# A spectral recurrence with 64 by 64 rotations in place of padded 128 by 128 ones

## The reference

```python
h = _ln(x, ln1_g, ln1_b)
spec = jnp.einsum('bsd,fd->bsf', h, W_to)            # W_to: (64, 128)
real, imag = (spec[..., :32], spec[..., 32:])
decay = sigmoid(log_decay); omega = tanh(frequencies) * 0.1
c, s = cos(omega), sin(omega)
def step(carry, u):                                  # 64 steps in time, 32 sequences at once
    sr, si = carry[0] * decay + u[0] * 0.1, carry[1] * decay + u[1] * 0.1
    nr = clip(sr * c - si * s, -10.0, 10.0)
    ni = clip(sr * s + si * c, -10.0, 10.0)
    return ((nr, ni), (nr, ni))
_, out = scan(step, zeros, (real, imag))
x2 = x + einsum('bsf,df->bsd', concat(out), W_from) * 0.1
return x2 + (gelu(_ln(x2, ln3_g, ln3_b) @ W_ffn1.T + b_ffn1) @ W_ffn2.T + b_ffn2) * 0.1
```

## Time and profile before

| | |
|---|---|
| runs | 3461.35, 3450.01, 3452.66 us; median 3452.66 |
| profiled execution | 3455.96 us, its span 3454.1 us |
| mean granted clock of TensorE | 0.879 |
| busy over the span | PE 79%, PEld 51%, DVE 63%, ACT 44%, POOL 12% |
| the loop over the time steps | 298.4 to 344.7 us of the span |

### The profile page before, as it was taken

One profiled execution on the slowest core, in us unless ns is written; L12 is line 12 of the kernel. 1 busy time (PEld: TensorE's weight loads), 2 busy tenths in 40 slices (PEclk: granted clock), 3 DMA queues, 4 the chain that ended last, 5 costly groups with the idle time before them and its releaser, 6 DMA issues. The chain is left out here.

```text
span 3454.1 us, 66228 instructions
## 1 busy us (share of the span) xinstructions
PE 2724.6 (79%) x26806; PEld 1744.5 (51%) x26806; DVE 2180.4 (63%) x6743; ACT 1514.6 (44%) x2755; POOL 410.8 (12%) x313
## 2 busy tenths in 40 slices
PE   7887543796997899999999999999479757887633
PEld 4656442454665355555555555555245425664422
DVE  4444403575111289999999999996578643445776
ACT  3441311463333245555555555553389422444521
POOL 2320011340000000000000000000059400002200
PEclk9998776797999589999999999996699867999866
DMA  7750041000000101001001000100022102550000
GB/s 164 185 126 10 18 127 28 7 3 15 13 19 23 29 20 30 21 21 30 21 21 29 23 21 22 30 2 1 7 77 98 37 0 68 130 138 20 9 0 12
DMA packets 206592, 142.78 MB, mean 41 GB/s; under 512 B 11778, under 2 KB 195045, under 8 KB 206256
## 3 DMA queue, kind: packets, MB, share of 16 engines
q1 hardware_dynamic: 205264, 136.70, 14.9%
q0 software_dynamic: 1024, 1.85, 0.2%
HBM read 134.31 MB, written 4.46 MB: 40 GB/s over the span
## 5 line engine op out<-in xcount | busy, mean ns | idle before, releaser
L2863 DVE CUSTOM_DVE_ANT_0 L_xattn_junk<-L_xattn_ps_mx,L_xattn_shift 128x512 f32<-128x512 f32 (+1 forms) x1024 | 544.3, 568 | 114.9 <-issue 111.9
L2944 ACT ACTIVATE L_xattn_pT<-L_xattn_ps_st 128x512 f32<-128x512 f32 x768 | 416.9, 594 | 348.1 <-PE L_xattn_ps_st L2728 348.1
L2909 DVE TENSOR_TENSOR L_xattn_pT<-L_xattn_pT,L_xattn_capT 128x512 f32<-128x512 f32 (+1 forms) x896 | 542.0, 645 | 31.5 <-ACT L_xattn_pT L2944 26.6
L2741 PE MATMUL L_xattn_ps_mx<-L_xattn_kT,L_xattn_qb 32*128 32x512 f32 (+1 forms) x2048 | 513.4, 571 | 0.9 <-DVE L_xattn_tops L2863 0.4
L2728 PE MATMUL L_xattn_ps_st<-L_xattn_qb,L_xattn_kT 32*128 32x256 f32 (+1 forms) x3328 | 457.1, 389 | 0.0
L2728 PEld LDWEIGHTS L_xattn_ps_st<-L_xattn_qb,L_xattn_kT 32*128 32x128 f32 (+1 forms) x3328 | 310.4, 186 | 22.8
L2774 PE MATMUL L_xattn_ps_pv<-L_xattn_pT,L_xattn_v 128*17 128x128 f32 x6656 | 271.3, 283 | 0.0
L2774 PEld LDWEIGHTS L_xattn_ps_pv<-L_xattn_pT,L_xattn_v 128*17 128x17 f32 x6656 | 149.7, 98 | 170.6 <-DVE L_xattn_pT L2909 126.6
L1811 DVE SCALAR_TENSOR_TENSOR x<-L_ffn_ps_o,L_ffn_weights,x 128x128 f32<-128x128 f32 x128 | 36.0, 344 | 224.5 <-PE L_ffn_ps_o L1724 224.5
L2741 PEld LDWEIGHTS L_xattn_ps_mx<-L_xattn_kT,L_xattn_qb 32*128 32x128 f32 x2048 | 168.3, 189 | 12.4 <-DVE L_xattn_tops L2863 9.7
L2754 PE MATMUL L_xattn_ps_st<-L_xattn_less,L_xattn_ones_b 3*128 3x512 bf16 x768 | 167.1, 394 | 1.7 <-ACT L_xattn_pT L2944 1.4
(11 more groups left out here) (554 smaller groups left out, 5172.1 us busy)
## 6 DMA issues: line engine op xcount, KB each, us to landing
L_xattn_ctx<-in_ctx SPq DMA_DIRECT2D x96, 768.0 KB
L_attn_cc<-scratch_rows SPq DMA_DIRECT2D x32, 512.0 KB, 3.6
L_xattn_mask<-in_mask_keys SPq DMA_DIRECT2D x32, 400.2 KB, 7.1
L_ffn_w<-in_L_ffn_w SPq DMA_DIRECT2D x32, 256.0 KB, 3.0
L_ffn_w<-in_L_ffn_W SPq DMA_DIRECT2D x16, 256.0 KB, 3.1
L_xattn_mask<-in_mask_pairs SPq DMA_DIRECT2D x32, 100.1 KB, 4.4
L_xattn_ctx<-in_ctx SPq DMA_DIRECT2D x96, 32.5 KB
scratch_in<-L_ffn_zero SPq DMA_DIRECT2D x1, 1024.0 KB, 5.1
```

Source lines behind the costliest of these rows:

```text
L2741: last = nc.tensor.matmul(mx[:, w % 3, to:to + width], qb[n % 3][32 * g:32 * g + 32, 2 * (p % 2):2 * (p % 2) + 2, :].rearrange("p h q -> p ...
L2863: last = nc.vector.tensor_tensor_reduce(out=junk[:, w % 3, to:to + width], in0=mx[:, w % 3, to:to + width], in1=shift[:, k0:k0 + width], s ...
L2909: nc.vector.tensor_tensor(x, x, capT[0:k, j[0]:j[1], :].unsqueeze(2).broadcast_to([k, j[1] - j[0], 4, S]), ALU.min)\
L2944: nc.scalar.activation(pT[b % HELD][:, :, gi, :], st[:, w % 3, :].rearrange("p (c k) -> p c k", c=2), ACT.Exp)\
```

## The change

F2 becomes 64, so that `rot_u` and `rot_z` are 64 by 64, the states, inputs and projections live on 64 partitions, and the five transfers take only the unpadded part. The fillers become matmuls of the 64 by 64 corner of the identity with itself, four for each step as before.

```diff
-    F2 = P
+    F2 = P // 2
@@
-            sp.dma_start(wto[:, :], a[f"{name}_W_toT"]).then_inc(gains, 16)
-            sp.dma_start(raw[:, 0:1], a[f"{name}_decay"]).then_inc(angles, 16)
-            sp.dma_start(raw[:, 1:2], a[f"{name}_freq"]).then_inc(angles, 16)
-            sp.dma_start(halves[:, :], a["c_halves"]).then_inc(angles, 16)
-            sp.dma_start(freq[:, :], a["c_freq"]).then_inc(angles, 16)
-            sp.dma_start(wfrom[:, :], a[f"{name}_W_fromT"]).then_inc(loaded, 16)
+            sp.dma_start(wto[:, :], a[f"{name}_W_toT"][:, 0:F2]).then_inc(gains, 16)
+            sp.dma_start(raw[:, 0:1], a[f"{name}_decay"][0:F2, :]).then_inc(angles, 16)
+            sp.dma_start(raw[:, 1:2], a[f"{name}_freq"][0:F2, :]).then_inc(angles, 16)
+            sp.dma_start(halves[:, :], a["c_halves"][0:F2, :]).then_inc(angles, 16)
+            sp.dma_start(freq[:, :], a["c_freq"][0:F2, :]).then_inc(angles, 16)
+            sp.dma_start(wfrom[:, :], a[f"{name}_W_fromT"][0:F2, :]).then_inc(loaded, 16)
@@
                 for _ in range(SPARE):
-                    nc.tensor.transpose(turn[:, 0, 0:P], c.ident[:, :], c.ident[:, :])
+                    nc.tensor.matmul(turn[0:F2, 0, 0:F2], c.ident[0:F2, 0:F2], c.ident[0:F2, 0:F2], start=True, stop=True)
```

## The result

The changed kernel takes 3481.77 us (median of nine runs, 3463.59 to 3483.67) against 3452.66 (nine runs, 3436.34 to 3461.35). The ratio is 1.008, its 95% interval 1.0056 to 1.0104: slower, by more than the 0.3% that the measurement tells from nothing, and 1.8 us from the 3480.0 forecast.

The account below looks back on a forecast made before the run. At the low clock the fillers' weight loads, not the dependent chain, were taken to bound the loop: 22.2 + 1.9 + 3.2 = +27.3 us on 3452.66 us gave 3480.0 us, range 3458 to 3496.

Parts of the forecast that it names:

- The clock in the loop: Recurrence loop of the spectral layer: small passes in one quarter leave TensorE's granted clock at 0.50 (1.2 GHz) all through.
- B: Rival: the clock stays high in the loop, period 0.61 us, 7.0 us less, 3445.7 us in all; chance 0.08.
- PEclk 0.50 from 265 to past the loop: Sign expected in the profile after: granted clock at 0.50 from 265 us, ahead of the loop, until past it.
- The period: Each of 64 loop steps: ten weight loads of 0.107 us make 1.07 us, +22.2 us over the loop.
- C: Rival: low clock, but fillers make one pass each instead of two; period 0.75 us, 3459.7 us in all; chance 0.05.
- D: Rival: load and stream do not overlap within one quarter; period 2.03 us, 3541 us in all; chance 0.05.
- The chain at the low clock: Loop step's load, matmul, clip and semaphore without the fillers' queue: 0.75 us, including 0.03 us more matmul latency.
- L1257, +1.9: Projection ahead of the loop: all eight passes at the low clock, 0.853 us each, +1.9 us.
- L1263, no change: Inputs ahead of the loop: eight passes stay 0.86 us apart at both clocks because of the strided moving operand.
- L1280, +3.2: Matmuls and adds behind the loop: pairs cost 0.213 us at the low clock, +3.2 us.
- The MLP, "warms up as now, I assume": MLP behind the stage: full-size matmuls assumed to warm up the clock as before, no term in the sum.
- The range: Whole kernel, 3458 to 3496 us: down to the one-pass-filler rival and up over the main forecast.

Follow-up runs that it names:

- e6: Changed kernel with its four fillers spread over the four quarters of the array, 256 streamed columns of hT each; 3447.2 us, ratio 0.9974 to the kernel before.
- e7: Changed kernel with its four fillers spread over the four quarters of the array, 64 streamed columns of hT each; 3458.1 us in one run.
- e3: Kernel before with its padded 128 by 128 rotations, fillers replaced by four 64 by 64 matmuls; 3510.8 us, ratio 1.0164 to the kernel before.
- e1: Changed kernel with two 64 by 64 fillers per step in place of four; 3456.9 us, ratio 1.0004 to the kernel before.
- e4: Changed kernel without any fillers; 3456.5 us, ratio 1.0005 to the kernel before.
- e8: Kernel before with its padded 128 by 128 rotations and no fillers; 3470.1 us, ratio 1.0041 to the kernel before.
- e2: Changed kernel with its 64 by 64 rotations, fillers again four full 128 by 128 transposes; 3500.3 us, ratio 1.0134 to the kernel before.
- e9: Changed kernel with its 64 by 64 rotations and eight full 128 by 128 transposes as fillers; 3495.7 us in one run.

## Why the prediction was right, point by point

- **The clock in the loop.** Forecast 0.50 throughout, measured 0.50 throughout. B is out: a PE without a gap, in one quarter, was left at 1.2 GHz. The reading that carried it was the earlier trace rows, and the experiments add what the earlier trace rows alone couldn't: the same tile size on four quarters with 256 columns (e6) has 1.00, the same passes with 64 columns (e7) 0.50, and small fillers let even a clock fall that starts the loop at 1.00 (e3).
- **How the clock got there: wrong, without a price.** The sign "PEclk 0.50 from 265 to past the loop" did not come. The clock was at 1.00 from 288 to 295 us and fell during L1263. The prediction had the mean of the earlier trace rows, 0.80 over 290 to 298.4, and not the fall and rise in it; that the loop starts low is right by L1263 and not, as it says, by L1257.
- **The period.** Ten loads of 0.107 us were forecast as 1.07; it is 1.067, and with eighteen 1.92. The term of the sum, +22.2, measured +22.0. C is out (512 records for 256 calls), and so is D.
- **The chain at the low clock.** Forecast 0.75 us, measured 0.719 (e1, e4). The 0.03 added for latency isn't there. The forecast didn't hang on it, but C, had it come, would have been priced 2 us too high.
- **L1257, +1.9: wrong.** It measured -0.2. The step that failed is that half the output columns would leave the clock low: it rose during L1257 (0.79 granted over 286 to 291), as before. In that stretch all 128 rows work, on 64 columns. Its passes went 0.85 us apart at 0.50 and 0.43 at 1.00.
- **L1263, no change: right,** 7.04 against 7.10 us, with the clock falling during it (0.62). The passes are 0.86 us apart in both kernels and at both clocks. The reason given, the stride, is argued: L1257, of the same 512 columns without one, does follow the clock.
- **L1280, +3.2:** +3.4.
- **The MLP, "warms up as now, I assume":** +1.1 us, not in the sum. With the missing 1.9 the two nearly cancel: 27.3 forecast, 26.1 measured for the stage.
- **The 1.8 us between forecast and median: in part luck.** The medians lie 29.1 us apart and the stage explains 26.1 of them; the other 3 lie in stages that the change doesn't touch, and a forecast from the stage alone could as well have missed by them. The sums hold but for roundings: (1.91 - 0.41) / 7 is 0.214, and 1.11 us a period would be +24.7.
- **The range.** Its lower part was meant for C, and what filled it was something else: two of nine runs lie at 3464, by the clock at the end of L2_xattn. The forecast gave later warm-ups "a few us"; between the profiled executions they make 14.7 in one stage and 11.1 in another.

The rule of the Trainium skill (TensorE: Matmul & The Clock Gate, "The mechanism", its list of what overlaps) that a load overlaps a running matmul only where the row groups differ does not agree with the step of the changed kernel: in one quarter, 64 columns loaded and 64 streamed cost 0.107 us a pass together. Either alone costs about that at the low clock: 64 more columns in each of two loads cost 0.22 us (e8 against e4), and 64 of the 512 columns that L1257 streams in 0.85 us are 0.107. That loads for other quarters go at the same time, as e7 shows, agrees with its picture of tiles working at once. The rule of the Trainium skill on the same page ("Why this matters for your kernels") that continuous work gives the full clock is contradicted by 68 us of continuous work at 0.50.

## What to carry to other kernels

A filler that is meant to hold TensorE's clock has to be judged by the granted clock of its stretch, not by whether the engine looks busy; if the clock is low with it, it brings nothing, and where it queues ahead of the next real instruction, taking it out gives the time back (22 us here). Shrinking a matmul to a quarter of the array made up for the low clock here and no more; it was a gain over the kernel before only with fillers of the same tile size on the other quarters too (e6), where their loads don't queue ahead of the chain's, and with full-size fillers it cost the pauses. Before a difference of 10 us in a kernel like this is believed, look in which stage of the profile it lies.

## What the runs showed of the hardware that was not expected

- Two changes between 64 by 64 and 128 by 128 matmuls in a period cost 0.32 and 0.33 us at 1.2 GHz (e2, e3) and 0.28 at 2.4 GHz (e9).
- Weight loads for one quarter follow each other 0.107 us apart at 1.2 GHz; ten of them, eight spread over four quarters, fit a period of 0.719 us (e7).
- A chain of two 64-column loads, matmul and clip at 1.2 GHz takes 0.719 us, one of 128-column loads at 2.4 GHz 0.723: the low clock cost the small rotation nothing against the padded one at the high clock.
- L2_xattn, which no run changed, takes 1307 us in two profiles and 1321 or 1322 in nine, by when the clock falls at its end. That moves a run of the whole kernel by 0.4%, more than the gain of e6.
